# A four-layer sequence model on one core: in the gated stage of the first layer, rows are normalised by another engine, one step earlier

## The reference

```
x  = x + L0_attn(layernorm(x))
# inside L0_attn, for the stage looked at here:
h    = layernorm(layernorm(x)) * gamma0 + beta0     # rows normalised, then turned
v    = h @ in_w[:, INNER:2*INNER]   + in_b[...]
gate = h @ in_w[:, 2*INNER:3*INNER] + in_b[...]
z    = silu(v) + sigmoid(gate) * y                  # y: output of the convolution, INNER = 256
out  = z @ out_w + out_b
# and the residual: the kernel keeps x in SBUF and builds  x + layernorm(x) + out  in place
```

## Time and profile before

| what | value |
|---|---|
| median of 3 runs | 3242.28 us (3238.45 to 3243.86) |
| the profiled execution's own time | 3245.29 us |
| its span, first to last instruction | 3243.2 us |
| busy over the whole span | PE 79%, DVE 66%, ACT 50%, POOL 24% |
| mean granted TensorE clock | 0.91 |
| the gated stage | from 270.6 to 393.5 us of the span |

### The profile page before, as it was taken

One profiled execution on the slowest core, in us unless ns is written; L12 is line 12 of the kernel. 1 busy time (PEld: TensorE's weight loads), 2 busy tenths in 40 slices (PEclk: granted clock), 3 DMA queues, 4 the chain that ended last, 5 costly groups with the idle time before them and its releaser, 6 DMA issues. The chain is left out here.

```text
span 3243.2 us, 69838 instructions
## 1 busy us (share of the span) xinstructions
PE 2553.1 (79%) x20225; PEld 1822.0 (56%) x20225; DVE 2129.7 (66%) x4755; ACT 1631.4 (50%) x3623; POOL 764.2 (24%) x1097
## 2 busy tenths in 40 slices
PE   4657859989988786999459999997676999984191
PEld 2334543449877533999237777767443666653180
DVE  5967875237778633777756666657876888855086
ACT  1646513332254443667535666652553777764063
POOL 0000100000000176555432222200251222211670
PEclk7889979999999898999779999998888999997595
DMA  3095100111190211222594566500086566521133
GB/s 104 0 213 143 46 13 20 35 43 49 36 172 0 78 53 51 71 69 67 171 243 53 72 72 70 69 6 1 1 263 68 72 72 72 72 25 45 52 100 111
DMA packets 316152, 241.10 MB, mean 74 GB/s; under 512 B 27069, under 2 KB 297837, under 8 KB 315693
## 3 DMA queue, kind: packets, MB, share of 16 engines
q1 hardware_dynamic: 288248, 202.91, 31.6%
q0 software_dynamic: 19072, 28.28, 3.0%
q10 hardware_dynamic: 8704, 8.39, 0.9%
HBM read 139.83 MB, written 96.51 MB: 73 GB/s over the span
## 5 line engine op out<-in xcount | busy, mean ns | idle before, releaser
L2619 ACT ACTIVATE h_pt<-h_ps 128x384 f32<-128x384 f32 (+1 forms) x1024 | 543.5, 545 | 278.1 <-PE h_ps L2528 143.5
L2365 DVE TENSOR_REDUCE h_nm<-h_ps 128x4 f32<-128x1024 f32 (+1 forms) x448 | 539.2, 1218 | 153.9 <-PE h_ps L2499 62.3
L1900 POOL DMA_INDIRECT results<-e_y,e_ykey x208 | 217.0, 1043 | 162.6 <-DVE e_y L1889 143.5
L1857 DVE TENSOR_SCALAR e_wt<-w 128x1156 f32 (+1 forms) x208 | 141.2, 680 | 166.1 <-PEq L1626 87.7
L2547 PE MATMUL h_ps_o<-h_pt,h_vp 128*32 128x256 f32 (+1 forms) x4096 | 246.8, 358 | 1.3 <-ACT h_pt L2619 1.3
L1947 ACT ACTIVATE e_hid<-e_ps_h,e_wt 128x128 f32<-128x128 f32 x688 | 201.3, 369 | 13.4 <-PE e_ps_h L1921 8.8
L2533 PE MATMUL h_ps<-h_sq,h_sk 128*128 128x256 bf16 x1024 | 193.4, 275 | 9.2 <-ACT h_pt L2619 4.3
L1929 PE MATMUL e_ps_o<-e_wt,e_hid 128*128 128x128 f32 x1376 | 192.4, 279 | 4.8 <-DVE e_y L1889 4.8
L1921 PE MATMUL e_ps_h<-e_hT,e_wt 128*128 128x128 f32 x1376 | 195.1, 281 | 0.6 <-ACT e_hT L1942 0.3
L2470 PE MATMUL h_ps<-h_sk,h_sq 128*128 128x256 bf16 x1024 | 156.1, 276 | 42.6 <-DVE h_identb L2347 36.6
L1704 POOL DMA_INDIRECT sorted_rows<-e_row,e_pos x128 | 124.6, 974 | 256.2 <-DVE e_row L1682 218.3
(11 more groups left out here) (457 smaller groups left out, 6249.7 us busy)
## 6 DMA issues: line engine op xcount, KB each, us to landing
h_sk<-k_stack SPq DMA_DIRECT2D x192, 128.0 KB
q_stack<-p_parts SPq DMA_DIRECT2D x64, 256.0 KB, 3.0
h_sq<-q_stack SPq DMA_DIRECT2D x64, 256.0 KB
sorted_rows<-pad SPq DMA_DIRECT2D x26, 520.0 KB, 10.6
e_xt<-sorted_rows SPq DMA_DIRECT2D x104, 130.0 KB, 2.2
e_got<-results SPq DMA_DIRECT2D x24, 512.0 KB, 4.7
k_stack<-p_parts SPq DMA_DIRECT2D x32, 384.0 KB, 3.0
b_tz<-ktab SPq DMA_DIRECT2D x32, 256.0 KB, 7.1
```

Of the source, the lines that this page charges most:

```text
L1857: dve.tensor_scalar(wt[j % 4][:, :], w[:, :, :].rearrange("p e w -> p (e w)")[:, ds(at, wc)], 1.0, None, ALU.mult).then_inc(e_w.sem, 1)
L1900: gp.indirect_dma_start(ys[:, :], bass.IndirectOffsetOnAxis(ap=key[m // 4][:, m % 4:m % 4 + 1], axis=0), y[m][:, :], None).then_inc(return ...
L2365: dve.tensor_reduce(to, got, AX, ALU.max, negate=True).then_inc(s["mx"].sem, 1)
L2619: act.activation(pt[g % 2][:, j, :], ps_2[:, h % 2, 0:SW], ACT.Exp, scale=scale).then_inc(s["ex"].sem, 1)
```

## The change

The four operations that normalise a unit's rows leave DVE and go to ACT. There they are `activation(Identity, scale=rstd2, bias=shift)` with a new column `c_shift` = -mean * rstd2, computed once by DVE; ACT starts after three chained DVE operations and no longer after two. `c_nrm` becomes three buffers, so ACT may write unit n once unit n-3 is turned. Every other work moves one step later relative to the rows: on DVE `added` has lag 4 and `gated` lag 2 (3 and 1 before), on PE `project`, `turn` and `project_out` have lags 2, 1 and 3 (1, 0 and 2 before), on ACT `gated` has lag 2 and `keep` lag 1 (1 and 0 before), while `grown` stays at lag 1. POOL's bias for unit n waits for z of unit n and no longer for the rows of unit n+2.

```diff
-            nrm = sb("c_nrm", [P, UT, P], stack=st)
+            nrm = [sb(f"c_nrm{j}", [P, UT, P], stack=st) for j in range(S)]
+            shift = sb("c_shift", [P, NT], stack=st)
...
-                k_set = n_chain[0] + 2
+                k_set = n_chain[0] + 3
...
+                    link(dve, dve.scalar_tensor_tensor(shift[:, :], mean[:, :], -1.0, rstd2[:, :], ALU.mult, ALU.mult))
...
-                    def normed(n, j, r):
-                        norm_tiles(dve, fr_c.nrm, nrm, x_res, n * UT, UT, rstd2, fr_c.tps.last(n, 1))
...
-                    staggered(dve, NU, S, (0, normed), (3, added), (1, gated))
+                    staggered(dve, NU, S, (4, added), (2, gated))
...
                         gp.wait_ge(*c_grown.now(n, 1))
-                        if not isinstance(n, int) or n + 2 < NU:
-                            gp.wait_ge(*fr_c.nrm.now(n + 2, 1))
+                        gp.wait_ge(*c_z.now(n, CB))
...
-                        turn_tiles(pe, fr_c.tps, ps_t[:, 0, :], nrm, UT, fr_c.nrm.now(n, 1), fr_c.hT.last(n, 1))
+                        turn_tiles(pe, fr_c.tps, ps_t[:, 0, :], nrm[j], UT, fr_c.nrm.now(n, 1), fr_c.hT.last(n, 1))
...
-                    staggered(pe, NU, S, (1, project), (0, turn), (2, project_out))
+                    staggered(pe, NU, S, (2, project), (1, turn), (3, project_out))
...
+                    def normed(n, j, r):
+                        act.wait_ge(*fr_c.tps.ago(n, 1, S))
+                        for t in range(UT):
+                            tile = ds(n * UT + t, 1)
+                            ins = act.activation(nrm[j][:, t, :], x_res[:, tile, :].rearrange("p o d -> p (o d)"), ACT.Identity,
+                                                 scale=rstd2[:, tile], bias=shift[:, tile])
+                        ins.then_inc(fr_c.nrm.sem, 1)
...
-                    staggered(act, NU, S, (1, gated), (0, keep), (1, grown))
+                    staggered(act, NU, S, (2, gated), (0, normed), (1, keep), (1, grown))
```

## The result

| kernel | median, us | runs | ratio to before, 95% interval |
|---|---|---|---|
| before | 3243.86 (3238.45 to 3246.33) | 5 | |
| changed | 3260.89 (3256.29 to 3261.73) | 5 | 1.0051 (1.0036 to 1.0065) |

The changed kernel is 17.0 us slower. The forecast of slower was right, the size was not: +9.8 was worked out, and 3260.9 lies above the range that ended at 3257.

The account below looks back on a forecast made before the run. DVE (6.99 us a unit) was taken to bound the stage before, the ACT-PE ring (7.37) after. Start +2.6, middle +11.4 and end -4.2 gave +9.8 us, so 3252 us, range 3243 to 3257.

Parts of the forecast that it names:

- a ring of 5.83 us: Gated stage, ACT and PE waiting on each other from c_hT to c_hT: 5.83 us, under DVE's 6.99 a unit.
- The rows are added whole: On ACT, rows stand outside its waits for PE, so their 1.54 us lengthen each unit from 5.83 to 7.37 us.
- A table load costs 0.83 on the ring: ACT's loop in the gated stage: each of three table loads adds 0.83 us, 2.5 us in all.
- In the steady ring PE is idle 7.37 - 5.9 = 1.5 us at a time: PE between units: idle 1.5 us, too short to lower its clock, so no cost was taken.
- The last output product: PE at the stage's end: 1.95 us at the high clock after about 2 us idle; 3.68 if cold, as a bound.
- first column to c_hT of unit 1: Stage's start, from DVE's first column: c_hT of unit 1 begins 2.6 us later than before.
- c_hT of unit 1 to that of unit 15: Stage's middle: 13 x 7.37 + 5.83, plus 2.5 for loads and 2.0 for clock, 106.1 us; 11.4 more than before.
- c_hT of unit 15 to the next stage: Stage's end: 12.7 us in place of 16.9, because DVE is no longer behind ACT; 4.2 us given back.
- The cold start of unit 1: PE idle 3.9 us before unit 1's projections, taken as at the lower clock: 2.0 us more, once.
- The busiest engine sets the pace, so the gaps close: Rival, gated stage: the engine with most work paces it and ACT's idle gaps close, 9.2 us saved, 3233; chance 0.12.
- Much slower: Rival: PE's 1.5 us gap lowers its clock in every ring, 26 us more, 3278; chance 0.04.
- The bias: POOL's bias, started with DVE's last sum: costed at nothing, with 1.4 us of DVE slack per unit to cover it.

Follow-up runs that it names:

- e5: Changed kernel with the rows back on DVE and POOL's bias again released by rows, new lags and three buffers kept: 0.9994 of before, stage 122.1 us.
- e9: Kernel before with ACT's steps of the gated stage written out, one table load left of five: 1.0001 of before, stage 120.8 us.
- e1: Changed kernel with ACT's rows moved behind c_hT of the unit before, inside ACT's wait for PE's products: 0.9977 of before, stage 113.7 us.
- e8: Changed kernel run again, nothing altered: 1.0047 of before, stage 135.6 us.
- e10: Changed kernel with POOL's bias no longer waiting for DVE's last sum, only for the growing of x: 1.0054 of before, stage 135.8 us.
- e7: Kernel before run again unchanged, for a second profile: stage 123.3 us.
- e6: Changed kernel with the rows behind c_hT on ACT and ACT's steps written out, one table load: 0.9960 of before, stage 108.9 us.
- e4: Changed kernel with the rows back on DVE; three buffers, new lags and the bias' new release kept: 1.0017 of before, stage 132.6 us.
- e2: Changed kernel with ACT's steps of the gated stage written out, one table load left of four: 1.0013 of before, stage 126.5 us.
- e3: Changed kernel with two extra unneeded products on PE ahead of each wait for c_hT: 1.0029 of before, stage 132.3 us.

## Why the prediction was right or wrong

**DVE paces the middle, and a ring of 5.83 us lies under it.** Shown. e5 keeps DVE's pace, and e9's first three rings run at 5.8.

**The rows are added whole, 5.83 + 1.54 = 7.37.** The ring is 7.34 in the trace, and e1 is the proof: same work, other place, 6.02.

**A table load costs 0.83 on the ring.** It costs 0.77 in its own unit. The gap of 1.30 from load to sigmoid stands here too (302.65; the next sigmoid at 303.94). What was missed is the second effect, below.

**"In the steady ring PE is idle 7.37 - 5.9 = 1.5 us at a time, less than the 2.31 that left the clock up. I take no cost there."** This is the step that failed. For plain rings it holds (1.42 and 1.41 before 325.06 and 340.51, never a long ring there). But a table load lengthens PE's gap to 2.2 us, and I had priced the load without asking what it does to PE. And I had taken one start, 2.31 us idle and a clock of 1.00, for a rule. In the changed kernel the clock fell behind two of three such gaps, 1.70 us each; in e8 and e10 also behind two of three. The last output product (3.12 and not 1.95, after 2.16 us idle) is the same mistake at another place; there the forecast had at least named the cold price of 3.68 as a bound. Together these are 4.6 us of the stage. Smaller terms that came out below the forecast hide about 1.7 of it.

The stage's sum against the trace (the last term ends with the first operation of the next stage):

| term | forecast, us | measured, us |
|---|---|---|
| first column to c_hT of unit 1 | 14.0 | 13.7 (269.63 to 283.29) |
| c_hT of unit 1 to that of unit 15 | 106.1 | 108.5 (to 391.74) |
| c_hT of unit 15 to the next stage | 12.7 | 13.6 (to 405.34) |
| sum | 132.8 | 135.7 |

The cold start of unit 1 was forecast at 2.0 and is 1.70. So the middle is out by two long rings (3.4), less the smaller terms (0.3 for the first, 0.2 for the loads, 0.5 for rings a little shorter than 7.37), and the end by 1.2 for the last product less 0.3.

**This step alone doesn't carry the time out of the range.** The measured 3260.9 is 8.8 us above the forecast, and the stage has 2.8 of them (12.6 against 9.8). With the stage as measured the forecast would have been 3255, still inside. Another 1.6 us is the median of before, 3243.9 over five runs and 3242.3 over the three that the forecast started from. The other 4.4 lie outside the stage, to which the forecast gave nothing. So the upper end of the range, 3257, left no room for these either.

**What remains.** The stage explains 12.6 of 17.0 us in the first pair and 12.4 of 15.2 in the second. By the intervals of the ratios the whole difference is 11.7 to 21.1 us in the first pair and 10.7 to 19.5 in the second, so the stage alone lies within both, and the rest isn't clear of noise. In the first profile the statistics behind the stage are 1.2 us longer as well, PE being at the lower clock (7.02 us for twelve instructions, 5.80 before); in e8 they take 4.11, so that part is chance. Of the other stages the changed kernel's profiles are about 3 us longer in all, on the chip of e7 and e8 (span less stage 3121.3 against 3118.2). e6 has that too and e5 has not; on the other chip e10, with the rows on ACT, has the shortest rest of all, and e9, with the rows on DVE, the next. Two profiles of one kernel differ by 2 to 2.5 us in this rest (3120.1 and 3118.2 before, 3123.8 and 3121.3 changed). So no order by the edit is shown in the sum.

In single stretches there is one. Three later stretches between statistics stages, whose operations are the same in all these kernels, fall into two groups over all twelve profiles, by where this stage's rows stand. With the rows on DVE (five profiles) and on ACT (seven), the second to the third takes 493.7 to 495.4 us and 495.5 to 497.1, the third to the fourth 161.9 to 162.4 and 163.3 to 165.6, the eighth to the ninth 566.6 to 568.3 and 562.3 to 564.3. The first two are longer and the last is shorter, by nearly as much, so it doesn't explain the 3 us. Why an edit here moves them stays open.

**The rivals.** "The busiest engine sets the pace, so the gaps close" fell as forecast: gaps of 0.62 and 0.45 stayed. Its time was within reach all the same: e6 is 12 us under before. It needed both things, DVE unloaded, since with the rows a unit costs DVE 6.99 us, and the ring opened, since without that it costs 7.34. The rule of the Trainium skill ("Perfetto Trace Analysis", "Optimizing Scalar/DVE Operations"), that work may go to the scalar engine when DVE is saturated, held in e1 and e6 (stage 113.7 and 108.9 us) and failed in the changed kernel (135.7). Between e1 and the changed kernel the difference is one exchange of two steps. "Much slower" named the right mechanism and put it in every ring, where it was in three, one of them forecast.

**The bias.** It was costed at nothing and cost nothing (e10). e4 and e5 showed that with rows on DVE the same release costs 10.5 us of stage (132.6 against 122.1 in e5).

## What to carry to other kernels

Before moving work to an engine with idle time, find what its idle time waits for, and put the work inside that wait: between the operation that starts the other engine's work and the one that needs its result. Outside of it, the work lengthens the ring by its full time, even while every engine has slack. When a stall of one or two microseconds is added to such a ring, ask also how long it makes TensorE's gap, and keep the slower clock in the range.

## What the runs showed of the hardware

- For PE's idle gaps of 2.2 to 3.2 us in this stage the length didn't decide whether the clock fell. Behind the nine table loads on the ring in the three profiles of the changed order (the changed kernel, e8, e10) PE was idle 2.20 or 2.21 us, and the clock fell six times and stayed up three, with the same work around. In the first profile the granted clock was 0.60 from 308 to 312 and 1.00 from 333 to 337. The last output product, after 2.16 us idle, took 3.12, 3.27 and 3.61 us in these three profiles and 2.05 in e2 and e3. After 2.71 us (e3) the clock was down, 0.65; after 2.77 (e7) and 3.20 (e2) it was up, 1.00. After the 1.4 us of the plain rings it stayed up every time, and after up to 1.88 us in e4 as well.
- Four `TENSOR_SCALAR` of 128x128 on DVE took 2.10 us under a 1.27 us `TENSOR_TENSOR` of POOL, and 1.11 without. The Trainium skill ("SBUF — State Buffer", "Who interferes with whom") says that such an operation can take the port pair shared with GpSimd and is then blocked while GpSimd holds it; the trace agrees, with 1.0 us of delay. The sum that reads PSUM (L802, 0.68 to 0.69) and the statistics (L345, 0.98 to 1.00) were not slowed by the same bias.
- In a hardware loop on ACT whose steps use Identity and Sigmoid, each round has one table load of 1.28 us, ahead of its first sigmoid. The steps written out behind the loop use the same two functions and have none. Written out as a whole (e2), the stage has one load in place of four.
